# A transposed context and transposed weights from memory, and the attn blocks of a gated cross-attention kernel set two by two

## What is computed

```python
qh = (layernorm(x) @ Wq)                    # 16 heads of 64
kh, vh = ctx @ Wk, ctx @ Wv                 # 1444 keys, 16 heads of 64
attn = softmax(qh @ kh.T / 8)               # 100 x 1444 for each head
x = x + tanh(g_xattn) * ((attn @ vh) @ Wo + bo)
z = layernorm(x)
h = silu(fp4_linear(z, w_gate)) * fp4_linear(z, w_up)       # 352 wide
x = x + tanh(g_ffn) * fp4_linear(h, w_down)
```

## Time and profile before

| | |
|---|---|
| median of 3 runs | 571.11 us (570.98 to 574.01) |
| the profiled execution | 572.5 us, its span 570.7 us |
| TensorE busy | 534.2 us, 94% |
| VectorE busy | 433.4 us, 76% |
| ScalarE busy | 311.2 us, 55% |
| GpSimd busy | 272.2 us, 48% |
| granted clock of TensorE, mean | 0.97 |

### The profile page before, as it was taken

The page is one execution under the profiler, slowest core; times in us unless marked ns, Lnnn a source line. Parts: engine busy times, 40 slices in busy tenths (PEclk is TensorE's granted clock), DMA queues, the critical chain, the costliest instruction groups (busy, mean ns, idle before and its releaser), DMA issues.

```text
span 570.7 us, 8404 instructions
## 1 busy us (share of the span) xinstructions
PE 534.2 (94%) x2841; PEld 333.0 (58%) x2841; DVE 433.4 (76%) x769; ACT 311.2 (55%) x731; POOL 272.2 (48%) x251
## 2 busy tenths in 40 slices
PE   5779999999999999999999999999999999999832
PEld 4555565666656565656566565656566565656421
DVE  2768876779786887779796887779787887776745
ACT  3444564666565754566565755566565755546411
POOL 4007427292735456292735456282735365284700
PEclk9789999999999999999999999999999999999975
...
DMA packets 27898, 9.45 MB, mean 17 GB/s; under 512 B 24016, under 2 KB 27600, under 8 KB 27856
## 3 DMA queue, kind: packets, MB, share of 16 engines
...
...
## 4 chain that ended last, share of the span: by engine, by line
PE 82%; DVE 10%; issue 3%; ACT 3%; POOL 1%; DMA 1%; SPq 0%; POOLq 0%; ACTq 0%; DVEq 0%
PE attn L807 24%; PE scores L793 16%; PE ring L746 12%; PE scores L794 11%; PE ring L760 5%; PE ring L753 4%; DVE max L915 3%; PE ring L725 3%; PE ring L732 2%; DVE acc_v L935 2%; PE ring L766 2%; ACT q_hh L583 1%; PE ring L774 1%; PE ring L749 1%; DMA x_in<-in_x 1%
## 5 line engine op out<-in xcount | busy, mean ns | idle before, releaser
L648 ACT ACTIVATE probs<-scores 120x400 f32<-120x400 f32 (+1 forms) x384 | 186.5, 504 | 193.0 <-PE scores L794 190.2
L915 DVE TENSOR_REDUCE max<-ring 116x1 f32<-116x482 f32 (+1 forms) x336 | 205.1, 653 | 57.7 <-PE ring L746 54.2
L513 POOL TENSOR_TENSOR acc_p<-acc_p,probs 120x800 f32<-120x800 f32 x79 | 152.7, 1934 | 71.7 <-ACT probs L648 65.8
L807 PE MATMUL attn<-probs,ctx_n 120*64 120x400 f32 (+1 forms) x768 | 171.8, 526 | 0.0
L793 PE MATMUL scores<-q_hh,k_hl 128*120 128x400 f32 (+1 forms) x384 | 153.5, 400 | 1.2 <-DVE q_ls L917 1.2
L793 PEld LDWEIGHTS scores<-q_hh,k_hl 128*120 128x120 f32 (+1 forms) x384 | 70.2, 183 | 125.6 <-ACT probs L648 72.0
L794 PE MATMUL scores<-q_ls,k_h 71*120 71x400 f32 (+1 forms) x384 | 133.9, 349 | 0.0
L746 PE MATMUL ring<-k_hl,q_hh 128*116 128x482 f32 (+1 forms) x336 | 119.5, 411 | 5.7 <-DVE k_hl L911 2.3
L794 PEld LDWEIGHTS scores<-q_ls,k_h 71*120 71x120 f32 (+1 forms) x384 | 70.9, 185 | 4.2
L746 PEld LDWEIGHTS ring<-k_hl,q_hh 128*116 128x116 f32 (+1 forms) x336 | 58.2, 182 | 16.6 <-DVE max L915 7.0
L807 PEld LDWEIGHTS attn<-probs,ctx_n 120*64 120x64 f32 (+1 forms) x768 | 38.1, 135 | 46.4 <-issue 34.4
...
## 6 DMA issues: line engine op xcount, KB each, us to landing
...
ctx_n<-in_ctx SPq DMA_DIRECT2D x16, 1.0 KB
...
```

The costliest lines, as they stand in the source:

```text
L513: pool.tensor_tensor(acc_p[0:r, t.g % 2, :], left, probs[0:r, c % PROBS, :], ALU.add).then_inc(sum_p, 1)
L648: act.activation(probs[0:r, c % PROBS, k * HALF:(k + 1) * HALF], scores[0:r, slot % SCORE_BANKS, 0:HALF], ACT.Exp).then_inc(probs_full, 1)
L807: mm = pe.matmul(attn[64 * i:64 * i + C, k, 0:HALF], ctx_n[0:r, par, c, 0, :], probs[0:r, c % PROBS, k * HALF:(k + 1) * HALF], start=(j == ...
L915: dve.tensor_reduce(max3[0:rows, tile, part:part + 1], src[0:rows, 0:MAXC[part + 1] - MAXC[part]], AX.X, ALU.max).then_inc(free, 1)
```

## The change

The context comes from memory a second time, transposed and with its keys in the order of the chunks (`ctxT`); the three weights come transposed. The transposes of context and weights on TensorE and what copied them out of the ring are gone. ScalarE copies `ctxT` in two parts into `k_hl` and `k_h1` (`copy_k`), and VectorE subtracts the high part from `ctxT` (`split_k`); both now read SBUF. The context for the attn blocks is loaded once, in longer pieces. The attn blocks get a table, `PV_SLOTS`: blocks 1 and 2, 6 and 7, 8 and 9, 10 and 11 stand in the same slot, one right behind the other, and the last four are later than before. The maxima begin at slot 8 (even groups) or 5 (odd groups), and are up to three to a slot. `q` moves to slot 1 and its four copies to slots 1 to 3, `shift` from slot 20 to 21, `sum` and `proj` differ by the parity of the group, the scaling of the heads is spread over slots 7 to 10, and the other tables shift by a slot or a few.

```diff
+KC = [0, M // 2, M]
...
-MAX_SLOTS = {1: 1, 2: 1, 4: 1, 5: 2, 7: 3, 8: 2, 10: 2, 11: 2, 12: 1, 13: 2, 14: 1, 15: 1, 16: 1, 17: 1}
-FFN_SLOTS = {2: ('zT', 0), 4: ('gate', 0), 6: ('up', 0)}
-DOWN_SLOTS = {2: ('hT', 0), 3: ('hT', 1), 5: ('down', 0)}
+MAX_SLOTS = [{8: 3, 9: 2, 10: 3, 12: 3, 13: 1, 14: 1, 16: 2, 17: 2, 18: 2, 19: 1, 20: 1}, {5: 3, 7: 1, 8: 1, 9: 2, 10: 3, 13: 2, 14: 2, 16: 2, 17: 3, 19: 2}]
+MAX_TILES_SLOT = [20, 19]
+SHIFT_SLOT = [21, 21]
+FFN_SLOTS = {1: ('zT', 0), 3: ('gate', 0), 5: ('up', 0)}
+DOWN_SLOTS = {4: ('hT', 0), 5: ('hT', 1), 7: ('down', 0)}
 LAST_FFN_SLOTS = {**FFN_SLOTS, 19: ('hT', 0), 20: ('hT', 1), 22: ('down', 0)}
-W_SLOTS = {slot: ("wT", i) for i, slot in enumerate(LAST_FFN_SLOTS)}
-POST_SLOTS = {6: ('sum', 0), 8: ('proj', 0), 10: ('proj', 1)}
-CTX_SLOTS = {14: ('ctx', 0), 15: ('ctx', 1), 18: ('ctx', 2)}
-XT_SLOT = 20
-MAX_TILES_SLOT = 17
-SHIFT_SLOT = 20
-
-
-LN2_SLOTS = [12, 13]
+W_SLOTS = {slot: ("wT", i) for i, slot in enumerate((2, 4, 6, 19, 20, 22))}
+POST_SLOTS = [{6: ('sum', 0), 9: ('proj', 0), 10: ('proj', 1)}, {7: ('sum', 0), 8: ('proj', 0), 10: ('proj', 1)}]
+XT_SLOT = 21
+LN2_SLOTS = [12, 14]
 LN2_APPLY_SLOT = 17
-Z_SLOTS = [19, 19, 20, 21, 21, 21, 22, 22, 22]
-SIGMOID_SLOTS = [5, 6]
-H_SLOTS = [18, 19, 19, 20, 21, 21, 22, 22, 23]
+Z_SLOTS = [17, 20, 20, 21, 21, 21, 21, 21, 22]
+SIGMOID_SLOTS = [5, 7]
+H_SLOTS = [12, 17, 18, 18, 19, 20, 21, 21, 23]
 LAST_H_SLOTS = [7, 8, 9, 10, 11, 12, 13, 14, 16]
-ADD_LAG, LAST_ADD_SLOT = 3, 0
+ADD_LAG, LAST_ADD_SLOT, ADD_LAST_SLOT = 3, 0, 1
+PV_SLOTS = [9, 11, 11, 12, 16, 17, 20, 20, 23, 23, 28, 28]
+COPY_SLOTS = [6, 7]
+Q_SLOT = 1
+Q_COPY_SLOTS = [1, 2, 3, 3]
+Q_LO_SLOTS = [2, 2]
+HEAD_SLOTS = [7, 7, 7, 8, 9, 9, 10, 10]
+LN1_SLOTS = [0, 1, 2]
+CTX_COPY_SLOTS = [7, 17, 17, 18]
+K_LO_SLOTS = [16, 18]
+POOL_AT = {'ln1': 1, 'ln2': 6, 'swiglu': (0, 3, 4), 'heads': 5}
...
-    if pre and slot == 0:
+    if pre and slot == Q_SLOT:
         keys += [("q", 0)]
...
-    if g % 2 == 0 and g + 2 < GROUPS and slot in CTX_SLOTS:
-        keys += [CTX_SLOTS[slot]]
-    if g >= 1 and slot in POST_SLOTS:
-        keys += [POST_SLOTS[slot]]
+    if g >= 1 and slot in POST_SLOTS[g % 2]:
+        keys += [POST_SLOTS[g % 2][slot]]
...
-START = [("wkT", 0), ("wqT", 0), ("xT", 0), ("A", 0), ("ctx", 0), ("q", 0), ("ctx", 1)]
-BETWEEN = {1: ('ctx', 2), 4: ('wqT', 1), 7: ('A', 1), 9: ('wvT', 0), 13: ('vo', 0), 14: ('vo', 1), 16: ('vo', 2), 20: ('vo', 3)}
+START = [("xT", 0), ("A", 0), ("q", 0), ("A", 1)]
+BETWEEN = {8: ('vo', 0), 11: ('vo', 1), 14: ('vo', 2), 17: ('vo', 3)}
...
-        ctx_n = sb("ctx_n", [128, 2, CHUNKS, 2, C])
+        ctx_n = sb("ctx_n", [128, 2, CHUNKS, C])
+        ctxT = sb("ctxT", [C, M])
...
             def load_ctx(b, par):
-                for i in range(2):
-                    sp.dma_start(ctx_n[0:PFULL, par, :, i, :], ctx_in[b, 0:PFULL * CHUNKS, :].rearrange("(p c) d -> p c d", c=CHUNKS)).then_inc(ctx_loaded[par], 16)
-                    sp.dma_start(ctx_n[PFULL:PFULL + 1, par, 0:EXTRA, i, :], ctx_in[b, PFULL * CHUNKS:M, :].rearrange("(p c) d -> p c d", c=EXTRA)).then_inc(ctx_loaded[par], 16)
+                sp.dma_start(ctx_n[0:PFULL, par, :, :], ctx_in[b, 0:PFULL * CHUNKS, :].rearrange("(p c) d -> p c d", c=CHUNKS)).then_inc(ctx_loaded[par], 16)
+                sp.dma_start(ctx_n[PFULL:PFULL + 1, par, 0:EXTRA, :], ctx_in[b, PFULL * CHUNKS:M, :].rearrange("(p c) d -> p c d", c=EXTRA)).then_inc(ctx_loaded[par], 16)
...
+            def load_qk(k):
+                heads = slice(4 * k, 4 * k + 4)
+                for r in range(2):
+                    rows = slice(64 * r, 64 * r + C)
+                    sp.dma_start(wkT[rows, heads, r, :], WkT[rows, heads, :]).then_inc(qk_in[k], 16)
+                sp.dma_start(wqT[:, heads, :], WqT[:, heads, :]).then_inc(qk_in[k], 16)
+
             load_x(0, 0)
-            load_ctx(0, 0)
+            load_qk(0)
+            sp.dma_start(ctxT[:, :], ctxT_in[0, :, :]).then_inc(ctxT_loaded, 16)
...
+            load_qk(1)
+            load_ctx(0, 0)
+            for i in range(2):
+                sp.dma_start(wvT[:, :, i, :], WvT).then_inc(wvo_in, 16)
...
+                    sp.wait_ge(k_hi_done, 4 * t.batch(1))
+                    sp.wait_ge(k_lo_done, 2 * t.batch(1))
+                    sp.dma_start(ctxT[:, :], ctxT_in[t.batch(1), :, :]).then_inc(ctxT_loaded, 16)
...
+            def copy_q(t, step):
+
+                half, r = (t.g + 1) % 2, step // 2
+                bank, n = t.ring(("q", 0))
+                if step == 0:
+                    act.wait_ge(ring_full[bank], n)
+                cols, rows = slice(r * HALF, (r + 1) * HALF), slice(64 * (step % 2), 64 * (step % 2) + C)
+                act.activation(q_hh[rows, half, cols], ring[64 * r:64 * r + C, bank, 0:HALF], ACT.Copy).then_inc(q_hi_done, 1)
+
+            def copy_k(t, step):
+
+                part, par = step // 2, t.parity(1)
+                cols = slice(KC[part], KC[part + 1])
+                if step == 0:
+                    act.wait_ge(ctxT_loaded, 16 * t.batch(2))
+                act.activation((k_hl, k_h1)[step % 2][par][0:C, cols], ctxT[:, cols], ACT.Copy).then_inc(k_hi_done, 1)
+
+            def scale_head(t, h):
+
+                i, k = h % 4, h // 4
+                bank, n = t.ring(("proj", k))
+                if i == 0:
+                    act.wait_ge(ring_full[bank], n)
+                if h == 0:
+                    wait_reads(act, (t, ("sum", 0)))
+                    if t.g >= 2:
+                        act.wait_ge(head_done, t.count(4, -4))
+                op = act.activation(head_out[0:N, h, :], ring[0:N, bank, i * D:(i + 1) * D], ACT.Copy, scale=rsum[0:N, h:h + 1])
+                if i == 3:
+                    op.then_inc(ring_free[bank], 1)
...
-                    if t.g >= 1 and slot in (1, 3):
-                        copy_attn(t, slot // 2)
+                    if t.g >= 1 and slot in COPY_SLOTS:
+                        copy_attn(t, COPY_SLOTS.index(slot))
+                    for step in [i for i in range(4) if Q_COPY_SLOTS[i] == slot and t.g + 1 < GROUPS]:
+                        copy_q(t, step)
+                    for step in [i for i in range(4) if CTX_COPY_SLOTS[i] == slot and t.g % 2 == 0 and t.g + 2 < GROUPS]:
+                        copy_k(t, step)
+                    for h in [i for i in range(HG) if HEAD_SLOTS[i] == slot and t.g >= 1]:
+                        scale_head(t, h)
...
-                elif kind == "ctx":
-                    par = t.parity(1)
-                    if k == 0:
-                        pe.wait_ge(ctx_loaded[par], 64 * t.fills(1))
-                    for c in range(4 * k, 4 * k + 4):
-                        r, a = CROWS[c], COFF[c] - COFF[4 * k]
-                        mm = pe.transpose(dst[:, a:a + r], ctx_n[0:r, par, c, :, :].rearrange("p i d -> p (i d)"), ident[0:r, 0:r])
...
+                    if t.g % 2 == 0:
+                        pe.wait_ge(k_hi_done, 4 * t.batch(1))
...
+                if i == 0 and t.g % 2 == 0:
+                    pe.wait_ge(ctx_loaded[par], 32 * t.fills())
...
-                    if slot % 2 == 0:
-                        i = slot // 2 - 2
-                        if i >= 0:
+                    for i in range(CHUNKS):
+                        if PV_SLOTS[i] == slot + SLOTS and t.g >= 1:
+                            attn_pair(t, i, 1)
+                    for i in range(CHUNKS):
+                        if PV_SLOTS[i] == slot:
                             attn_pair(t, i, 0)
-                        elif t.g >= 1:
-                            attn_pair(t, i + CHUNKS, 1)
...
+            def split_k(t, part):
+
+                par = t.parity(1)
+                cols = slice(KC[part], KC[part + 1])
+                dve.wait_ge(k_hi_done, 4 * t.batch(1) + (part + 1 if t.g < 0 else 2 * part + 1))
+                dve.tensor_tensor(k_hl[par][C:128, cols], ctxT[:, cols], k_hl[par][0:C, cols].bitcast(F32), ALU.subtract).then_inc(k_lo_done, 1)
+
+            def split_q(t, r):
+
+                half, (bank, n) = (t.g + 1) % 2, t.ring(("q", 0))
+                rows, cols = slice(64 * r, 64 * r + C), slice(r * HALF, (r + 1) * HALF)
+                if r == 0:
+                    dve.wait_ge(ring_full[bank], n)
+                dve.wait_ge(q_hi_done, t.count(4, 4 + 2 * r + 2))
+                op = dve.tensor_tensor(q_ls[0:C, half, cols], ring[rows, bank, 0:HALF], q_hh[rows, half, cols].bitcast(F32), ALU.subtract)
+                if r == 1:
+                    op.then_inc(ring_free[bank], 1)
...
-                elif kind == "ctx":
-                    par = t.parity(1)
-                    dve.wait_ge(k_hi_done, 3 * t.batch(1) + k + 1)
-                    a, b = COFF[4 * k], COFF[4 * k + 4]
-                    dve.tensor_tensor(k_hl[par][C:128, a:b], src[C:128, 0:b - a], k_hl[par][C:128, a:b].bitcast(F32), ALU.subtract).then_inc(free, 1)
...
+                if key == ("q", 0):
```

(36 more changed lines are left out.)

137 lines of the change are left out of this document (42 added, 95 removed).

## The result

The changed kernel takes 592.62 us (median of 4 runs, 588.83 to 593.88) where the kernel before took 571.71 beside it: a ratio of 1.035, with an interval of 1.029 to 1.041. It is slower by 21 us; 24 less were predicted, with a chance of 0.03 for slower. The profiled execution took 592.01 us with a span of 590.0. Further down, the runs of experiments 8, 10 and 12 fall into two clusters some 7 us apart (563.6 to 564.9 and 570.4 to 572.3 in run 8; 552 to 554 and 559 to 562 in the last two), for a reason that stays open, so that differences of their medians under that are not read.

A forecast was written before the change was run, and what follows sets the result against it. TensorE was taken as the bound; 3.95 us saved less 1.65 of waits gives 2.3 a pair, 16.1 over seven, plus 5.1 (start), 2.0 (group 0), 0.3 (end): 571.1 - 23.5 = 547.6 us. Range 536 to 560, the forecast's own 542 to 555.

The forecast's parts named there:

- What bounds the kernel: Whole kernel: TensorE bounds it, busy 94% of the span and 82% of the chain; VectorE is busy 76%.
- the price of a block: attn blocks on TensorE: a lone one takes 1.01 us; one that joins another saves 0.34 us.
- the ScalarE count: Copies on ScalarE: four of 722 columns replace six of some 480, 3.2 us against 3.4, so nothing won.
- Change 1 and 2: TensorE, per pair of groups: adjacent blocks save 2.7 us, dropped context transposes 1.25; together 3.95.
- (a): Slot 4 of even groups: scores wait 0.5 us for slot 2's exponential, delayed by ScalarE's copies of q.
- (b): Bare slots 14 and 15 of even groups, and head scaling in slot 7: new waits of 0.3 us together.
- (c): shift in slot 21 of even groups: TensorE waits some 0.45 us for the last maximum, VectorE standing about 0.7 for ScalarE.
- (d): Subtractions in slots 16 and 18, now with two SBUF inputs: GpSimd collisions cost 0 to 1.56 us each, taken as 0.4.
- Change 4: The start: earlier x load and no weight transposes end the reduces at 29.2 instead of 34.3 us, gain 5.1 (3 to 7).
- Change 5: Group 0: maxima begin only in slot 8; the group takes 30.6 instead of 32.6 us, gain 2.0 (0 to 4).
- D: Rival, odd groups: four h-chain links shut out by GpSimd's adds, TensorE waiting up to 5 us a pair; 583 us, chance 0.03.
- B: Rival: VectorE takes over through whole collisions with GpSimd, 1.65 to 3.3 us more a pair; about 563 us, chance 0.13.

The follow-up runs named there:

- run 8: Run 7's kernel with the four vo products moved from the start into slots 3 to 6 of group 0; 570.50 us, ratio 0.992.
- 10: run 9's kernel with all twelve attn blocks two by two; 556.74 us, ratio 0.968.
- run 12: The kernel of 10 with the second and third z links moved behind the shift's product on VectorE; 556.32 us, ratio 0.968.
- Run 7: run 6's kernel with one h link of the odd groups moved from slot 18 to 19; 570.44 us, ratio 0.997.
- Run 2: Changed kernel with one h link of the odd groups moved from slot 18 to 19, behind max_tiles; 582.55 us, ratio 1.019.
- run 9: run 8's kernel with group 0's two split_k moved from slot 16 to 21, behind max_tiles; 563.22 us, ratio 0.981.
- runs 1: Changed kernel with both split_k moved from slots 16 and 18 of even groups to slot 3 of the following odd group; 620.33 us, ratio 1.084.
- run 6: Changed kernel with even groups' key copies in slots 7, 12, 12, 17 and both split_k in slot 16; 575.34 us, ratio 1.003.
- Run 4: Changed kernel with useless matmuls on TensorE ahead of shift's wait, 8 in even groups and 5 in odd; 587.62 us, ratio 1.027.

## Why the prediction was wrong

**What bounds the kernel, the price of a block, the ScalarE count: right.** Double blocks take 1.56 us wherever the clock is full.

**Change 1 and 2, "TensorE loses 3.95 us a pair": over-sized.** Run 7's pair is 61.6 us with 0.92 us in idle rows (0.70 and 0.22), so 60.7 of work against 63.6: 2.9 saved, 1.1 less than forecast. Groups 6 and 7 of the two traces, each instruction counted from its start to the next one's without the waits, show where. The blocks take 1.0 us less, the transposes that are gone 1.2, the maxima matmuls 0.8 and the other ring users 0.5 less; but the scores matmuls take 0.7 more, where 8 x 0.18 = 1.4 less were due. What I left out: where a ring user other than a maxima matmul stood beside a block, the two shared one break in the stream of scores. The first scores matmul behind such a break takes 0.28 us to the next one instead of 0.18, and the last one ahead of a block 0.27. There are 27 such breaks in the pair before and 29 in run 7. Eight joined blocks should have left 19; ten ring users that now stand alone opened as many. At the 0.18 that I gave the two sides of a block that is 1.8 us, an estimate, beside the 2.1 that the scores show. No run moved a ring user back to a block to test it.

**Change 3 (a) and (b), 0.5 + 0.3: over-sized.** Slot 4 waits 0.22 us, not 0.5, and in groups 2 to 13 it is the only slot whose scores wait for `probs`.

**(c) and (d), 0.45 + 0.4: the step that failed first.** The waits for `maxes` are 1.76 and 1.11, 2.87 us a pair. I had named every part: `z` late by 0.7 (0.85), a subtraction up to 1.56 longer (1.22: 2.13 against 0.91), the h chain in the upper bound (1.49: 2.02 against 0.53). (The 14 maxima of (c) are 13 in the table of slots, so VectorE's 11.0 us there should have been 10.4; put right, (c) would have come out lower still.) Then I took the odds that "one of two should meet an add half way". But GpSimd's adds stand back to back there, 6.46 and 8.00 us, and the phase is the same in all groups: the second subtraction takes 2.12 or 2.13 in each of the six even groups, the first 0.90 or 0.91. Such a collision recurs at one price, that of its place, and the mean over all places is not it. Run 2, and group 13, show the cause for the odd groups, and run 9 for the wait of 6.31 in run 8's group 0; for the even ones runs 1 and 6 together show that the wait goes with the order of these steps, and that VectorE's total work doesn't make it, since run 6 has the same steps.

The 24 subtractions from PSUM before took 0.66 us on the mean, the 16 of after 1.46:

```profile
L905 DVE TENSOR_TENSOR k_hl<-ctxT,k_hl 64x722 fp32r<-64x722 f32 x16 | 23.3, 1459 | 4.3 <-ACT k_hl L570 3.9
```

By the Trainium skill (SBUF — State Buffer, Who interferes with whom), a VectorE instruction with two inputs in SBUF contends with a GpSimd instruction that reads SBUF, since its second input comes through the shared read interface. This trace agrees, with 2.13 us against 0.91. The same section of the Trainium skill has `tensor_scalar` too among the operations that can take the shared pair of ports, and run 12 is its case: 1.70 against 0.17.

**The clock: a term that was missing, and the largest.** I took full clock for granted since the earlier trace rows show 1.00. Behind each stand of 1.76 us the clock was at its lower level for a stretch, 1.4 us on one double block. Run 4 shows that it hangs on the stand. Three terms add up to the mean pair's 66.3: 60.7 of work, 2.9 of waits (16.1 us for `maxes` and 1.3 in slot 4, over six pairs), and 2.7 of half clock (the difference; an estimate from the mean granted clock of 0.96 from 108 to 495 us gives as much, 0.04 x 66.3). Against 63.6 that is 2.7 more, where I had 2.3 less. Of these 5.0 us a pair, 1.1 are TensorE's work, 1.2 the waits (1.65 in the forecast) and 2.7 the clock: with the work and the waits alone a pair would have taken its old 63.6.

**Change 4, the start, "29.2 instead of 34.3": wrong.** The last reduce ended at 34.5. The first one ran at 14.1, as I had it at 14.3, and `q` was on time. But I gave 1 us to the waits, and nothing to `vo` or to the clock. A `vo` of eight matmuls takes 2.08 us at half clock instead of 1.16, three maxima matmuls 1.55, and in that rhythm of 3.5 us VectorE stands 1.7. Run 8 shows that: without them the last reduce ends at 28.4 and the first scores stand at 30.6.

```profile
28.40 1.01 PE L751 MATMUL ring<-k_hl,q_hh 128*116 128x482 f32 x2
29.34 2.08 PE L718 MATMUL ring<-wo,wvT 64*128 64x128 f32 x8
31.34 1.95 PE L751 MATMUL ring<-k_hl,q_hh 128*116 128x480 f32 x4
34.91 0.54 PE L754 MATMUL ring<-ident,maxes 116*7 116x116 f32 x2 [1.61 <-DVE maxes L959]
```

Why the clock is low from 18 to 48 us, where before it was so from 17 to 24 and 37 to 44, is open: TensorE was busy nearly all the time, and no run was made for it.

**Change 5, group 0, "a gain of 2.0": wrong.** 3.9 us lost, 3.13 in one row, a maxima matmul waiting for a reduce behind a `split_k` of 2.47 and links of 2.47 and 1.87. The rest lies beside the half clock up to 48 us and was not taken apart. It is (d) again, in the group where VectorE has the weights' fp4 chain besides.

**The rivals.** D's mechanism, the h chain beside GpSimd's adds, was there with one link of the four. B's collisions were there in full and were priced at 1.65 to 3.3 us a pair. Neither had the clock, which made a loss of the two; even D's 583 us is 10 short. They have one cause, GpSimd's adds beside VectorE's two-input steps, and I gave them chances of 0.13 and 0.03 as if they were apart.
